# k's head stacks by ACT and POOL, another order of loads and first items, two groups per output bank, one burst of output matmuls per group: a decoder layer in fp32 on one core

## What is computed

```python
q = _rope(x @ wq.T); k = _rope(x @ wk.T); v = _rope(x @ wv.T)
qh, kh, vh = (t @ w.T + b for t, w, b in ...)          # in_proj, heads of 8
attn = softmax(where(causal, qh @ kh.T / sqrt(8), -inf))
x = layernorm(x + (attn @ vh) @ out_w.T + out_b)
q, k = apply_rope(x @ Wq.T + bq), apply_rope(ctx @ Wk.T + bk)
x = layernorm(x + (softmax(q @ k.T * scale) @ v) @ Wo.T + bo)
y = einsum('tei,ehi->teh', silu(h1) * h3, w2)          # h1, h3 of all 8 experts
x = layernorm(x + einsum('te,teh->th', expert_w, y))   # expert_w: top 2, others 0
```

## Time and profile before

| | |
|---|---|
| three runs | 287.84, 289.03, 289.09 us, median 289.03 |
| profiled execution | 290.4 us, its span on the core 288.3 us |
| mean granted TensorE clock | 0.975 |
| busy, share of the span | PE 262.7 us (91%), DVE 203.1 (70%), ACT 155.9 (54%), POOL 110.8 (38%) |
| the chain that ended last | PE 76%, ACT 7%, DVE 7%, issue 3%, DMA 3%, POOL 2% |

### The profile page before, as it was taken

One profiled execution on the slowest core, in us unless ns is written; L12 is line 12 of the kernel. 1 busy time (PEld: TensorE's weight loads), 2 busy tenths in 40 slices (PEclk: granted clock), 3 DMA queues, 4 the chain that ended last, 5 costly groups with the idle time before them and its releaser, 6 DMA issues.

```text
span 288.3 us, 4324 instructions
## 1 busy us (share of the span) xinstructions
PE 262.7 (91%) x1326; PEld 161.2 (56%) x1326; DVE 203.1 (70%) x603; ACT 155.9 (54%) x293; POOL 110.8 (38%) x175
## 2 busy tenths in 40 slices
PE   6478799999999899999999989999989999999980
PEld 2135656655655556667654666566656556565640
DVE  7639688897889988766573499835788854555464
ACT  1446135576789955867788747685342333432300
POOL 9950003413323353133743232025364455554531
PEclk9977799999999999999999999999999999999997
DMA  7920002000000400000212100000000000000002
GB/s 199 392 60 0 1 0 75 0 3 1 3 0 0 145 3 0 2 1 0 68 44 67 45 1 0 2 1 0 2 0 1 0 2 0 0 0 2 0 0 73
DMA packets 5797, 8.62 MB, mean 30 GB/s; under 512 B 720, under 2 KB 3280, under 8 KB 5648
## 3 DMA queue, kind: packets, MB, share of 16 engines
q1 hardware_dynamic: 4976, 7.14, 7.6%
q10 hardware_dynamic: 720, 0.95, 0.9%
q0 software_dynamic: 80, 0.26, 0.6%
HBM read 7.83 MB, written 0.52 MB: 29 GB/s over the span
## 4 chain that ended last, share of the span: by engine, by line
PE 76%; ACT 7%; DVE 7%; issue 3%; DMA 3%; POOL 2%; SPq 0%; POOLq 0%; DVEq 0%; ACTq 0%
PE psB L840 10%; PE psA L812 10%; PE psO L947 8%; PE psO L857 7%; PE psB L719 3%; PE psO L865 3%; DMA c<-c_dram 3%; PE psJ L876 2%; PE psO L868 2%; PE psA L720 2%; PE psA L721 2%; PE psA L719 2%; PE psB L721 2%; PE psB L720 2%; PE psJ L824 2%
## 5 line engine op out<-in xcount | busy, mean ns | idle before, releaser
L1230 DVE CUSTOM_DVE_ANT_0 junk<-psA,c 128x128 bf16<-128x128 f32 (+3 forms) x128 | 56.1, 486 | 5.8 <-PE psA L812 5.4
L690 POOL TENSOR_TENSOR gated<-silu,wbc 128x512 f32<-128x512 f32 x32 | 41.1, 1286 | 41.5 <-DVE hid L1344 30.1
L1047 ACT ACTIVATE prob<-psB 128x512 f32<-128x512 f32 (+1 forms) x88 | 47.6, 560 | 16.1 <-PE psB L840 15.0
L1101 ACT ACTIVATE silu<-psA 128x512 f32<-128x512 f32 x32 | 19.1, 598 | 44.6 <-PE psA L721 40.3
L1334 DVE SCALAR_TENSOR_TENSOR silu<-silu,psA 128x512 f32<-128x512 f32 x32 | 21.9, 684 | 27.8 <-ACT silu L1101 27.8
L812 PE MATMUL psA<-kst,qa 128*128 128x512 f32 (+1 forms) x88 | 39.8, 460 | 1.3 <-DVE kst L1165 1.2
L840 PE MATMUL psB<-qb,kst 128*128 128x512 f32 (+3 forms) x128 | 37.6, 337 | 1.0 <-ACT prob_more L1047 0.5
L1235 DVE TENSOR_REDUCE negm<-psA 128x3 f32<-128x462 f32 (+1 forms) x48 | 26.1, 579 | 10.3 <-PE psA L812 9.9
L947 PE MATMUL psO<-hid,w 128*128 128x512 f32 x64 | 33.1, 598 | 0.2 <-DVE hid L1344 0.2
L675 POOL TENSOR_SCALAR_AFFINE_SELECT prob<-prob 128x256 f32<-128x256 f32 x32 | 13.2, 413 | 50.3 <-ACT prob_more L1047 50.1
L1047 ACT ACTIVATE prob_more<-psB 128x512 f32<-128x512 f32 (+1 forms) x48 | 24.6, 530 | 12.1 <-PE psB L840 11.6
(11 more groups left out here) (150 smaller groups left out, 522.9 us busy)
## 6 DMA issues: line engine op xcount, KB each, us to landing
c<-w_dram SPq DMA_DIRECT2D x8, 256.0 KB, 2.8
w<-w_dram SPq DMA_DIRECT2D x1, 1024.0 KB, 4.9
c<-c_dram SPq DMA_DIRECT2D x1, 666.0 KB, 9.4
xT<-xt_dram SPq DMA_DIRECT2D x2, 256.0 KB, 6.0
x_tok<-x_dram SPq DMA_DIRECT2D x1, 512.0 KB, 10.0
out_dram<-x_tok SPq DMA_DIRECT2D x2, 256.0 KB, 2.3
wa<-wa_dram ACTq DMA_DIRECT2D x2, 192.0 KB, 5.5
wx<-wx_dram SPq DMA_DIRECT2D x1, 384.0 KB, 8.6
```

Source lines behind the costliest of these rows:

```text
L690: nc.gpsimd.tensor_tensor(gated[:, n % 2, :], silu[:, n % 2, :], wbc[:, (E * b + f // 2) % 2, :], ALU.mult).then_inc(s_sg, 1)
L1047: nc.scalar.activation(dst, psB[n % SIZE["B"]][:, 0:cols], ACT.Exp, scale=SCALE).then_inc(b_done[n % SIZE["B"]], 1)
L1101: nc.scalar.activation(silu[:, n % 2, :], psA[a % SIZE["A"]][:, :], ACT.Tanh, scale=0.5).then_inc(s_th, 1)
L1230: last = nc.vector.tensor_tensor_reduce(out=junk[:, p, cols], in0=psA[p][:, cols], in1=c32[:, C_MASK + S - width:C_MASK + S], scale=-1.0, ...
```

## The change

1. k's stacks. Unit 0 keeps its way as SK0 (ACT and DVE, 32 rows at a time). For the other seven, SK is one ACT copy of the whole bank into `kcomp` (two slots) and four POOL products of it with 0/1 columns (`C_HEAD`), which write all 128 rows of the four heads' slots, so that nothing has to be cleared. SC likewise. DVE has no part in them.
2. U(0,v) and the three U(1,w): an ACT copy into `rest` and the two products on POOL. U(0,q) and U(0,k) stay on DVE.
3. MP moves from POOL to DVE.
4. Loads: fr's selection matrices go last on ACT's queue, v's matrices and `c16` move to SP's queue, `brow` from POOL's to SP's. FR is five items. PE waits for the part of `fr` that it needs.
5. First items: U(0,v) is placed behind H(0,k), batch 1's U behind MT(0), CK behind U(1,v).
6. v's tiles hold v at column 16 of 32; a window of 32 columns that starts at 0 or at 16 puts a group's result in the upper or the lower 16 rows of each quarter and adds zeros to the other. Two groups share psO; POC and OT run once for the two (8 and not 16 times), and OT's DVE part is one reciprocal and two products.
7. PV is one item a unit (`BURSTS`): in stage 0 its 16 matmuls run in one go when the last mask is there, in stage 1 the four and the one for the last tokens.
8. `onorm` lies over the fr constants, some costs of the planner are others (latencies 0.16 to 0.21 us, maxima 0.077 + n/960), and the constants have four columns more.

```diff
+BURSTS = ((0, 1, 3, 2),), ((0, 1),)
+
+ROPE = {(b, w): "DVE" if (b, w) in ((0, "q"), (0, "k")) else "POOL" for b in range(B) for w in "qkv"}
+
+
+V_AT = 16
+
+
+def v_from(g):
+    return V_AT * (1 - g % 2)
...
+                late.append((ROPE[b, w] == "POOL" and 2 or 1, before))
+            deps = [("LOAD", (b,))]
+            if (b, w) == (0, "v"):
+                deps.append((("H", (0, "k")), 0))
+            if b:
+                deps.append((("MT", (0,)), 0))
+            if ROPE[b, w] == "DVE":
+                add("U", (b, w), [("PE", 0.86), ("DVE", 1.2)], deps, late)
+            else:
+                if copied:
+                    deps.append(copied[-1])
+                copied.append(("U", (b, w)))
+                add("U", (b, w), [("PE", 0.86), ("ACT", 0.5), ("POOL", 2.55)], deps, late)
         for w in "qk":
...
+            if u == 0:
+                add("SK0", (), [("PE", 0.46), ("ACT", 1.38), ("DVE", 1.52, 0)], [("H", (b, "k")), ("FR", (g,))])
+                continue
+
+            deps = [("SK", divmod(u - 2, NG))] if u >= 3 else []
+            late = [(2, (("B", (u - SLOTS, len(b_fills(u - SLOTS)) - 1)), 0))] if u >= SLOTS else []
+            add("SK", (b, g), [("PE", 0.46), ("ACT", 0.6), ("POOL", 3.0)], [("H", (b, "k")), ("FR", (g,))] + deps, late)
...
+        for k, kts in enumerate(BURSTS[st]):
+            deps = [("MK", (u, kts[-1])), ("VH", (b,))] if st == 0 else [("B", (u, exps_of(u, kts[-1])[-1])), ("CV", ())]
+            if g % 2 == 0 and k == 0 and u:
+                deps.append(("POC", (u // 2 - 1,)))
+            add("PV", (u, k), [("PE", 0.3 + sum((S - 128 * kt if st == 0 else S) / 600.0 for kt in kts))], deps)
+        if g % 2 == 0:
+            continue
+        p = u // 2
+        add("POC", (p,), [("ACT", 0.49)], [last_pv(u)] + ([(("OT", (p - 1,)), 0)] if p else []))
+        add("OT", (p,), [("PE", 0.44), ("DVE", 0.8)], [("POC", (p,)), ("LOAD", (3,))],
+            [(1, ("ONT", row(u - NG)))] if g == 1 and u >= NG else [])
...
-            sp.dma_start(c32[:, C_FR:C_MASK], c32_d[:, C_FR:C_MASK]).then_inc(s_fr, 16)
             sp.dma_start(c32[:, C_MASK:C_CQ], c32_d[:, C_MASK:C_CQ]).then_inc(s_mask, 16)
+            sp.dma_start(wa[:, 7:10, :], wa_d[:, 7:10, :]).then_inc(s_iv, 16)
...
+            sp.dma_start(brow[:, :, :], bass.AP(brow_d.tensor, 0, [[0, 128], [1, 512]])).then_inc(s_row, 16)
...
+            sp.dma_start(c16[:, :], c16_d).then_inc(s_c16, 16)
...
+                    nc.gpsimd.tensor_tensor(ab[:, n % 2, 0, :], rest[:, m % 2, :], c32[:, C_CA:C_CA + S], ALU.mult)
+                    nc.gpsimd.tensor_tensor(ab[:, n % 2, 1, :], rest[:, m % 2, :], c32[:, C_SA:C_SA + S], ALU.mult).then_inc(s_rope, 1)
+                elif kind == "SK":
...
+                    if u >= SLOTS:
+                        pool.wait_ge(s_b, FILL["B"]["B", (u - SLOTS, len(b_fills(u - SLOTS)) - 1)] + 1)
+                    for j in range(G):
+                        nc.gpsimd.tensor_scalar(kst[:, u % SLOTS, j, :], kcomp[:, u % 2, :], c32[:, C_HEAD + j:C_HEAD + j + 1], None,
+                                                ALU.mult).then_inc(s_km, 1)
+                elif kind == "SC":
+                    g, = args
+                    job_done(pool, "SC", g)
+                    for j in range(G):
+                        nc.gpsimd.tensor_scalar(kc[:, :, g, j, :], kcomp[:, g % 2, 0:B * SC].rearrange("p (b t) -> p b t", b=B),
+                                                c32[:, C_HEAD + j:C_HEAD + j + 1], None, ALU.mult).then_inc(s_kc, 1)
...
+                    kts = BURSTS[st][k]
...
-                            last = nc.tensor.matmul(po[32 * j:32 * j + 32, 128 * kt:S], v_sb[b][:, kt, G * g + j, :],
-                                                    prob_at(u, kt, j), start=kt == 0, stop=kt == 2, skip_group_check=True)
-                        if kt == 2:
-                            last.then_inc(s_pv, 1)
-                    else:
-                        fill_done(pe, "B", [("B", (u, k)) for k in exps_of(u, kt)])
-                        if kt == 0:
+                        if g % 2 == 0 and u:
+                            pe.wait_ge(s_po, u // 2)
+                    for kt in kts:
+                        if st == 0:
+                            pe.wait_ge(s_mk, masks(u, kt))
+                        else:
+                            fill_done(pe, "B", [("B", (u, n)) for n in exps_of(u, kt)])
+                        if st == 0 or kt == 0:
+                            v = (v_sb[b][:, kt, :, :] if st == 0 else vc_sb[:, b, :, :]).rearrange("p h c -> p (h c)")
                             for j in range(G):
-                                nc.tensor.matmul(po[32 * j:32 * j + 32, :], vc_sb[:, b, G * g + j, :], prob_at(u, 0, j),
-                                                 start=True, stop=False, skip_group_check=True)
+                                last = nc.tensor.matmul(psO[32 * j:32 * j + 32, 128 * kt:S], v_window(v, g, j), prob_at(u, kt, j),
+                                                        start=kt == 0 and g % 2 == 0, stop=st == 0 and kt == 2 and g % 2 == 1,
+                                                        skip_group_check=True)
                         else:
-                            nc.tensor.matmul(po[:, :], vblk[:, b, g, :, :].rearrange("p j c -> p (j c)"), prob_at(u, 1, None),
-                                             start=False, stop=True, skip_group_check=True).then_inc(s_pv, 1)
+                            first = 128 * g + v_from(g)
+                            last = nc.tensor.matmul(psO[:, :], vblk[:, b, :, :, :].rearrange("p g j c -> p (g j c)")[:, first:first + 128],
+                                                    prob_at(u, 1, None), start=False, stop=g % 2 == 1, skip_group_check=True)
+                    if k == len(BURSTS[st]) - 1:
+                        last.then_inc(s_pv, 1)
...
-            act.dma_start(wa[:, 7:10, :], wa_d[:, 7:10, :]).then_inc(s_iv, 16)
-            act.dma_start(c16[:, :], c16_d).then_inc(s_c16, 16)
+            act.dma_start(c32[:, C_FR:C_MASK], c32_d[:, C_FR:C_MASK]).then_inc(s_fr, 16)
...
+                    free(JOB[item], nc.scalar.activation(rest[:, m % 2, :], ps[:, :], ACT.Copy))
...
+                    ps = bank(JOB[item])
+                    if u >= 3:
+                        act.wait_ge(s_km, G * (u - 2))
+                    free(JOB[item], nc.scalar.activation(kcomp[:, u % 2, :], ps[:, :], ACT.Identity, bias=c32[:, C_ONE:C_ONE + 1]))
...
+                    p, = args
+                    act.wait_ge(s_pv, 2 * p + 2)
+                    if p:
+                        job_filled(act, ("OT", (p - 1,)))
+                    nc.scalar.activation(po_sb[:, :], psO[:, :], ACT.Copy).then_inc(s_po, 1)
...
+                    link(nc.vector.tensor_copy(rows[:, :, :, ROWS], negm[:, p, :, :]))
+                    nc.vector.tensor_tensor(rows[:, :, :, ROWS + 1], negm[:, p, :, :], rows[:, :, :, ROWS].bitcast(FP32),
+                                            ALU.subtract).then_inc(s_mp, 1)
...
-                                                  rec[:, u % 2, :, :].unsqueeze(3).to_broadcast([128, QT, G, HD]), ALU.mult)
+                    p, = args
+                    ps = bank(JOB[item])
+                    if p % 2 == 0 and p:
+                        job_filled(dve, ("ONT", divmod(p // 2 - 1, 2)))
+                    o = ps[:, :].rearrange("p (i j h c) -> p i j h c", i=QT, j=G, h=2)
+                    link(nc.vector.reciprocal(rec[:, p % 2, :], ps[:, :].rearrange("p (n c) -> p n c", c=V_AT)[:, :, HD]))
+                    sums = rec[:, p % 2, :].rearrange("p (i j h) -> p i j h", i=QT, j=G)
+                    for h in range(2):
+                        first = 32 * (p * 2 % NG + h)
+                        ins = nc.vector.tensor_tensor(onorm[:, :, first:first + 32].rearrange("p i (j d) -> p i j d", j=G), o[:, :, :, h, 0:HD],
+                                                      sums[:, :, :, h].unsqueeze(3).to_broadcast([128, QT, G, HD]), ALU.mult)
```

More of the change, by code:

```diff
@@ L43 @@
 C_ONE = C_MASK + S
-C_CQ = C_ONE + 4
+C_HEAD = C_ONE + 4
+C_CQ = C_HEAD + G
 C_SQ = C_CQ + S
@@ L137 @@
 }
-LATENCY = {"PE": 0.22, "ACT": 0.17, "DVE": 0.15, "POOL": 0.18, "SP": 0.1, "LOAD": 0.1}
+LATENCY = {"PE": 0.21, "ACT": 0.2, "DVE": 0.18, "POOL": 0.16, "SP": 0.1, "LOAD": 0.1}
 def tasks():
@@ L539, in layer_kernel @@
         s_pool = sem("s_pool")
+        ROPED = [("U", key) for key in ROPE if ROPE[key] == "POOL"]
         block = ctx.enter_context(nc.Block())
@@ L1182, in _ @@
                     bias = brow[:, 0, :].rearrange("p (h d) -> p h d", h=H).unsqueeze(1).to_broadcast([128, QT, H, HD])
-                    free(JOB[item], nc.vector.tensor_tensor(v_sb[b][:, :, :, 0:HD], tiles(ps[:, :]), bias, ALU.add))
+                    free(JOB[item], nc.vector.tensor_tensor(v_sb[b][:, :, :, V_AT:V_AT + HD], tiles(ps[:, :]), bias, ALU.add))
                 elif kind == "CK":
```

270 lines of the change are left out of this document (125 added, 145 removed).

## The result

| | before | after |
|---|---|---|
| median of the runs, us | 289.06 (287.84 to 290.25) | 302.56 (301.16 to 304.27) |
| ratio | | 1.047, 95% interval 1.04 to 1.054 |
| span of the profiled execution, us | 288.3 | 302.5 |
| POOL busy, us | 110.8 | 164.8 |
| first matmul of A, first exp, us | 21.27, 42.30 | 15.30, 33.93 |

The account below looks back on a forecast made before the run. PE was taken to bound the kernel from 42 us on, a latency chain the first 42 us. Start 8, PE 9, DVE and ACT 2 off, POOL and bursts 2 on: 290.4 to 273.4, less 1.4 for the median: 272 us, range 262 to 285.

Parts of the forecast that it names:

- POOL's product: Stacks and SC on POOL: a one-input 512-column product costs 0.8 us, bounds 0.6 and 1.29.
- rival D: POOL's queue: products at their upper price, 49.6 us, stand before masks or A, half showing on PE; 297 us, chance 0.09.
- POOL's queue: Masks waiting behind POOL's stacks, together with PV bursts outrunning ACT's and DVE's banks: adds 2 us, between 0 and 8.
- The start: First 42 us: first A near 16.5 us, first exp near 26; gain 10 us, 8 kept, bounds 3 and 12.
- rival B: Start not gained, because fr's load or bcol holds the first A where it is; 280 us, chance 0.10.
- PE's work: Stage 0: bursts and shared bank together spare PE 11.8 us, three quarters kept, 9 us, bounds 3 and 13.
- bursts: Stage 0: one PV burst a group spares 24 changes between tiles and whole array at 0.34 us, 8.2 us.
- the shared bank: Two groups in one output bank: OT's transposes made 8 times and not 16, 3.6 us of PE spared.
- rival A: ACT, DVE or POOL sets stage 0's pace, PE's savings become waits, only the start remains; 281 us, chance 0.19.
- DVE and ACT: DVE loses 14 us and ACT 10 us of work; worth 2 us in 42 to 110, between 0 and 5.
- The range: Whole kernel: 262 to 285 us at 0.8; bounds of the terms around the forecast given as 264 to 280.

Follow-up runs that it names:

- e1: Forms of POOL instruction, timed alone and beside DVE work, added at the end of e3's kernel; the stacks' 512-column product took 1568 ns alone.
- e3: Changed kernel with k's and the context's stacks back on ACT and DVE, written from PSUM: 284.1 us, ratio 0.9829 to before.
- e6: Changed kernel with POOL's stack products in the two-input form, same order and planned costs: 283.37 us, ratio 0.9777 to before.
- e4: Changed kernel with only the planner's costs of POOL's stacks and SC set to measured size (6.3 and 4.3 us): 293.49 us, ratio 1.0144 to before.
- e5: Changed kernel with POOL's stacks made by copies of 32 rows, slots cleared once at the start, planned costs kept: 279.0 us, ratio 0.9658 to before.
- e9: e5 with PV in four items a group in stage 0 and two in stage 1, no bursts: 274.42 us, ratio 0.9514 to before.
- e10: Changed kernel with all set back but the shared bank (fr's single-item copies and planner's small costs stay): 288.99 us, ratio 1.0018 to before.
- e7: e3 with PV in four items a group in stage 0 and two in stage 1, no bursts: 282.32 us, ratio 0.9756 to before.
- e8: Kernel before with only the bursts added, PV as one item a group: 290.01 us, ratio 1.0044 to before.
- e11: Kernel before, same order, without the output matmuls of kt = 1 in stage 0 (7.8 us of PE's work): 284.35 us, ratio 0.9848.
- e12: Kernel before, same order, without one of two stack and SC writes each on ACT and DVE (7.5 and 8.2 us): 281.06 us, ratio 0.9749.

## Why the prediction was wrong, step by step

**POOL's product, the step that failed.** "I take 0.8, by the copy of 208 columns in 0.35 and the select" took the price of a product from other kinds of instruction. Both neighbours are in fact cheap (the copy of 512 columns is 0.61, in e1, and the select 0.41); the product is not: it measured 1.57, and even the upper bound, a two-input row, was 0.28 us too low. The bound rested on the thought that one input can't cost more than two; e1 has 1.57 against 1.04. The Trainium skill, GPSIMD Engine Reference, section Engine selection (4.1), calls one-input work on this engine roughly line-rate, the thought behind my bound; the measurement decides against it for this form. Its Key points have the DVE about twice as fast, and for this product the runs agree: DVE's one-input write of 512 columns takes 0.75 us, on 32 rows from PSUM, POOL's 1.57. For a copy they agree less: POOL's is 0.61 and DVE's quickest 0.43, in e1. For the product that sentence, quoted for rival D, was the better guide.

**POOL's queue, the term that this price went into.** "I add 2 us, between 0 and 8." e3 puts it at 18.5 us; e6, with nothing but the price changed, takes 19 off. Rival D had the right mechanism and place, with a decision point of 16.5 us of wait, and was given 0.09. It had 49.6 us of products with half of them, 25 us, showing; there were 59.9, of which 18.5 showed, and part of these is the clock (above), which no rival had. That the time is still above its 297 lies on the other side: it set 17 us of gains against the loss, and without the stacks only 289.1 - 284.1 = 5 us of gain are there (e3). What neither had: the order is the planner's, so a wrong planned cost can be an error of its own, about 9 us in the one order tried (e4). The prediction said that its sum "goes by loads and not by places". The diff shows the planned 3.0 us, which my own upper price of 5.2 contradicted; what an order made for 3.0 does with 5.2 belonged among the rivals.

**The start.** The first A came at 15.30 (16.5 forecast), so rival B is out. The first exp came at 33.93 (26): with the stacks off POOL it is no sooner, 34.8 in e3, where DVE writes the stacks of groups 1 to 3 (4.6 us, between 16.2 and 23.8) ahead of the maxima; with copies on POOL it is 29.1 (e5) and 30.2 (e9). The gain kept, 8 us, was about right nevertheless: e10 and e7 differ by the start's order, U on POOL and MP on DVE, and by 289.0 - 282.3 = 6.7 us. In their profiled executions the first output matmul comes at 49.6 and at 42.5, at granted clocks of 0.86 and 0.96 up to there, so part of it is clock. (The prediction's "half of whose matmuls run at a lowered clock" is too much: a granted share of 0.88, between levels of 2.4 and 1.2 GHz, is by my estimate about a quarter of the time.) With the stacks on POOL at 1.57 us this gain is lost again: the first output matmul of the changed kernel comes at 52.3, before's at 49.5.

**PE's work.** "Three quarters = 9 us" measured zero, for bursts (e7, e8) and for the shared bank (e10), and -4.6 for the bursts beside cheap stacks (e9). The 0.34 us of a visit to the tiles is real, and the burst saves it. PE's microseconds do count in stage 0, by e11 about 4.9 for 7.8, so the error was not that PE's share of 65.0 of 68 us was read as load. It was to price little beside what the burst spares: the waits behind it were put at a quarter of the saving and the lower granted clock at nothing (e8), and with what stays open there all of the saving goes. For these terms rival A was the better forecast. Why the shared bank's 3.6 us don't arrive is not shown. The Trainium skill, TensorEngine Tiling (Array Packing), Key Properties, on the drain still agrees with the trace; the saving just doesn't reach the end.

**DVE and ACT.** "2 us for it, between 0 and 5" was made for stage 0, and there it was only a little small: half of the stacks' writes off both engines gives 3.0 us in the body of stage 0 (e12), and moving them to cheap copies on POOL, e7 to e9, 90.0 - 86.4 = 3.6 us. What it lacked is the start, where each gives more again (6.0 us in e12, clock included, and 42.5 - 38.5 = 4.0 from e7 to e9); in all they are worth 7.7 and 282.3 - 274.4 = 7.9 us. So PE's 9 came to 0, and DVE and ACT's 2 came to 8. That e5, the changed kernel with copies, is at 279.0 and within the range is in part luck: these two errors cancel.

**The range.** Its top, 285, left D out at 0.09. The bounds of the terms, added straight, give 259 to 291 and not 264 to 280, and even 291 is below the measured time, since POOL's term was bounded at 8 and came to 18.5. The price of 28 + 16 instructions of a form that no row showed deserved more.

## What to carry to other kernels

Before an instruction of a new form goes onto an engine many times, time that very form: on POOL, 128x512 costs 0.61 us as a copy, 1.04 as a two-input product and 1.57 as a product with a scalar, and in e6 the choice of form alone was worth 19 us. Where the order comes from a planner, give it the measured cost of the new item: with it, and no other change, half of this loss went. To learn what bounds a kernel, take some work off each engine in turn, without changing the order, and look not only at the end but at where along the order the time goes: e12's 7.7 us looked like the pace of stage 0 and were for the larger part its start. And a wait on PE can cost more than its length, by the granted clock behind it.
